# Splitting one VectorE product of a four-tile group into four products of one tile, in an edge-softmax kernel

## The reference, cut to what matters

```python
qkv = (h @ W_qkv + b_qkv).reshape(n, 3, H, DH)          # H = 8 heads of DH = 32
q, k, v = (qkv[:, 0], qkv[:, 1], qkv[:, 2])
score = jnp.einsum('ehd,ehd->eh', q[dst], k[src]) * SCALE
mx = jax.ops.segment_max(score, dst, num_segments=n)
ex = jnp.exp(score - mx[dst])
denom = jax.ops.segment_sum(ex, dst, num_segments=n)
attn = ex / denom[dst]
msg = attn[:, :, None] * v[src]
h_new = jax.ops.segment_sum(msg, dst, num_segments=n)
```

## Time and profile before

| | |
|---|---|
| time, median of 3 runs | 2125.84 us (2121.98 to 2130.7) |
| span of the profiled execution | 2134.3 us |
| stage with the attention's edges | about 1243 to 1900 us of the span |
| VectorE busy, share of the span | 72% |
| TensorE busy, share of the span | 83% |
| GpSimd busy, share of the span | 54% |

### The profile page before, as it was taken

The page is one execution under the profiler, slowest core; times in us unless marked ns, Lnnn a source line. Parts: engine busy times, 40 slices in busy tenths (PEclk is TensorE's granted clock), DMA queues, the critical chain, the costliest instruction groups (busy, mean ns, idle before and its releaser), DMA issues. The chain is left out here.

```text
span 2134.3 us, 41549 instructions
## 1 busy us (share of the span) xinstructions
PE 1761.5 (83%) x10388; PEld 1537.1 (72%) x10389; DVE 1539.6 (72%) x2788; ACT 1070.3 (50%) x2353; POOL 1160.5 (54%) x1169
## 2 busy tenths in 40 slices
PE   3699999999999989828973868888888888866278
PEld 3499999999999979728972756666666766645267
DVE  5388888888888845643545849899999898847622
ACT  1677777777777726403420145445455454316133
POOL 0376666666666601462443457777777777512112
PEclk7799999999999989758996989999999999867579
DMA  3443333333333312133323566666666666524310
GB/s 96 133 121 111 104 108 108 104 107 108 105 106 108 98 31 80 69 124 98 119 75 98 193 185 189 189 188 188 193 191 186 190 187 188 148 65 141 115 38 29
DMA packets 132538, 267.55 MB, mean 125 GB/s; under 512 B 24030, under 2 KB 75888, under 8 KB 132407
## 3 DMA queue, kind: packets, MB, share of 16 engines
q0 software_dynamic: 63456, 191.61, 30.7%
q1 hardware_dynamic: 68534, 73.21, 11.2%
q10 hardware_dynamic: 416, 1.18, 0.2%
HBM read 225.34 MB, written 42.50 MB: 125 GB/s over the span
## 5 line engine op out<-in xcount | busy, mean ns | idle before, releaser
L319 POOL DMA_INDIRECT e_rows<-h_table,e_idx x440 | 453.4, 1030 | 214.1 <-issue 106.3
L1740 POOL DMA_INDIRECT a_rows<-kv_table,a_idx x440 | 476.1, 1082 | 135.8 <-issue 128.9
L619 PE MATMUL e_w<-w2h,e_hidl 128*128 128x256 f32 x880 | 247.7, 304 | 2.9 <-DVE e_msg L704 2.9
L589 PE MATMUL e_agg<-e_msg,e_hot 128*128 128x256 f32 x880 | 246.1, 402 | 0.0
L1822 PE MATMUL a_q<-q,a_spread 128*128 x880 | 233.7, 407 | 6.5 <-ACT a_spread L1782 6.3
L620 PE MATMUL e_w<-w2l,e_hidh 128*128 128x256 f32 x880 | 226.4, 280 | 0.0
L1853 PE MATMUL a_agg<-a_rows,x 128*128 128x264 f32 x880 | 226.2, 402 | 0.0
L704 DVE TENSOR_TENSOR e_msg<-e_w,e_rows 128x1024 f32<-128x1024 f32 x110 | 134.7, 1224 | 93.4 <-PE e_w L623 93.4
L1775 ACT ACTIVATE a_apart<-iota_n,dst_rel 128x128 f32<-128x128 f32 x440 | 140.6, 391 | 112.9 <-PE a_agg L1853 112.8
L1822 PEld LDWEIGHTS a_q<-q,a_spread 128*128 128x128 f32 x880 | 166.2, 199 | 38.9 <-issue 12.8
L1853 PEld LDWEIGHTS a_agg<-a_rows,x 128*128 128x128 f32 x880 | 168.2, 200 | 24.7
(11 more groups left out here) (456 smaller groups left out, 4221.4 us busy)
## 6 DMA issues: line engine op xcount, KB each, us to landing
e_ea<-in_eaT SPq DMA_DIRECT2D x220, 64.0 KB
m_rows<-expert_rows SPq DMA_DIRECT2D x32, 272.0 KB, 2.7
e_rows<-h_table,e_idx POOLq DMA_INDIRECT x440
a_rows<-kv_table,a_idx POOLq DMA_INDIRECT x440, 3.7
q_ab<-expert_out SPq DMA_DIRECT2D x50, 128.0 KB, 3.3
kv_table<-q_kv SPq DMA_DIRECT2D x25, 256.0 KB, 2.2
u_stage<-in_m_w SPq DMA_DIRECT2D x16, 256.0 KB
x<-in_x SPq DMA_DIRECT2D x1, 3200.0 KB, 13.9
```

The costliest lines, as they stand in the source:

```text
L319: c.nc.gpsimd.indirect_dma_start(out=rows[:, g.slot8, j, :], out_offset=None, in_=table, in_offset=bass.IndirectOffsetOnAxis(ap=idx[:, g.s ...
L589: last = mm(bank(wins[j]), hot[:, g.slot4, t, :], msg[:, g.slot4, t, :], start=False, stop=False, skip_group_check=True)
L619: mm(w, hidl[:, g.slot, cols[k]], w2h[:, k, :], start=(k == 0), stop=False)
L1740: nc.gpsimd.indirect_dma_start(out=rows[:, g.slot * IG + j, 0:2 * D], out_offset=None, in_=c.kv_dram, in_offset=bass.IndirectOffsetOnAxis( ...
```

## The change

The one `tensor_tensor` over a group's four tiles (128 partitions x 4 x 256 elements) becomes a loop of four over one tile each (128 x 256). Operands, operation, type and place stay the same: it is in place, and the exponentials are read with a step of zero over the 32 elements of a head. The signal `s_msg` goes with the fourth. Nothing else is changed; lines behind it move down by four.

```diff
                         need(dve, s_dg, (s_ex, m.chunk + 1))
-                        ex = rows[:, four(m), 2 * D:ROW].rearrange("p t (h a) -> p t h a", a=1).broadcast_to([P, IG, H, DH])
-                        v.tensor_tensor(by_head(rows[:, four(m), D:2 * D]), by_head(rows[:, four(m), D:2 * D]), ex, ALU.mult).then_inc(s_msg, 1)
+                        for j in range(IG):
+                            tile = rows[:, m.slot * IG + j, :]
+                            values = tile[:, D:2 * D].rearrange("p (h d) -> p h d", h=H)
+                            ex = tile[:, 2 * D:ROW].rearrange("p (h a) -> p h a", a=1).broadcast_to([P, H, DH])
+                            last = v.tensor_tensor(values, values, ex, ALU.mult)
+                        last.then_inc(s_msg, 1)
                         ahead.fetch(i.then, "sums", m.n)
```

## The result

The changed kernel takes 2139.94 us in the median of 4 runs (2135.59 to 2141.53), against 2126.73 us (2121.98 to 2130.7, 4 runs) before: a ratio of 1.0059, 95% interval 1.0041 to 1.0077, so +12.5 us (8.7 to 16.4; the medians alone lie 13.2 us apart). The prediction was 2140 us, with 2130 to 2154 as its range.

A forecast was written before the change was run, and what follows sets the result against it. VectorE was taken to set the stage's pace, GpSimd close behind. 23.1 - 5.1 - 5.4 = +12.6 us, put at +14 for doubt in point 5; 2125.84 + 14 = 2140 us, range 2130 to 2154 us.

The forecast's parts named there:

- Points 1 to 3: VectorE's multiply in each group: three added instructions at 0.07 us each, 0.21 us a group, +23.1 us (20 to 26).
- Point 4: VectorE's wait for grow before L1903, once a chunk: the longer multiply covers it, -5.1 us.
- Point 5: VectorE's waits for gathered rows (all) and for queries and exponentials (half) go: -5.4 us (bounds 0 and -8.4).
- Point 6: TensorE's sums (L1848) come 0.21 us later each step; L1890 takes them later, so nothing new waits in the steady part.
- The period: Mean distance of the once-per-chunk marker L1928 (L1924 before): 22.8 to 22.9 us, against 22.34 us before.
- the stages ahead: Stages before and after the changed one: unchanged within 2 us in the profile.
- Rival A: Slack takes most of VectorE's added time; if all other waits vanished, a chunk takes 22.50 us: +4 to +10.6 us; 22%.
- Rival B: No overlap between the four multiplies on VectorE: durations count in full, +0.47 us a group, +47 us, 2173 us; 5%.
- Rival C: GpSimd falls behind if gathers are held through all four multiplies, not let in between: over +19, up to +30 us; 12%.
- the first reading: A gather meeting the first of four multiplies is held until the fourth ends; GpSimd needs 5.75 us a group, +18 us.
- Rival D: Faster: an added VectorE instruction costs under 0.04 us, freer gathers and covered waits outweigh it; down to -13 us, 2113 us; 4%.

The follow-up runs named there:

- the pair with fewer gathers: One multiply and four multiplies, each with the fourth tile of a group not gathered once the ring is full: -7.0 us and +12.3 us against before.
- light kernel: Kernel before, one multiply, with the fourth tile of a group not gathered once the ring is full (output partly wrong): 2121.2 us, ratio 0.9967.
- the move alone: Kernel before, one multiply, with the rescaling of the shared destination put behind the product of keys and queries: 2125.2 us, ratio 0.9992.
- two multiplies and the move: Against before: two multiplies of two tiles per group, and the rescaling put behind the product of keys and queries: 2112.93 us, ratio 0.9936.

## Why the prediction was right, step by step

- **Points 1 to 3, the price on VectorE** (0.21 us a group, 23.1 us): right. The trace shows 1.34 against 1.13 us, and eight multiplies fit the same 0.07 us per instruction.
- **Point 4, grow** (-5.1 us): right. The floor rose by 22.45 - 21.86 = 0.59 us and not by 4 x 0.21 = 0.84; in the pair with fewer gathers it rose by 0.69 (21.76 to 22.45). So 0.15 to 0.25 us per chunk were given back, and the forecast was 0.19. Price less grow was predicted as 18.0 us; that pair, in which almost no other wait is left to give, lies 19.3 us apart.
- **Point 5, the other waits** (-5.4 us): a good size, with a reason only half right. The light kernel shows that they were worth 7.0 us. I had said that only the waits for rows hang on the gathers, and had taken half of those for queries and exponentials by judgement. All but 0.5 us of them vanishes when gathers have room, even with VectorE as fast as before. I did not follow how a late gather turns into a wait for queries. For the exponentials the trace of before shows the way, over TensorE's clock. TensorE's matmul of L1811 waits once in a chunk for VectorE. Of 24 chunks, it waits 1.46 us or more in the 11 (1.20 or 1.21 us in 12 of the others) in which VectorE has waited for rows or queries just before. Behind 7 of these 11, and behind no other, the granted clock falls from full speed (2.4 GHz) to 0.50 of it (1.2 GHz) for about 4 us. The exponentials pass over TensorE next, and VectorE's 7 waits for them (3.1 us) are in these 7 chunks. One of them, TensorE's wait, its next eight matmuls, the clock in two windows (the third figure from the end), and VectorE's wait at the end:

```profile
1364.28 0.62 PE L1811 MATMUL a_misc<-carried,heads_of_row 8*128 8x34 f32 x2 [1.82 <-DVE carried L1941]
1364.83 3.42 PE L1822 MATMUL a_q<-q,a_spread 128*128 x8
```

```profile
1358.00:1363.00 5.00, 4.09 (x23) 3.11 (x21) 3.78 (x6) 2.68 (x9) 3.78 (x5) 1.00 0.61 184
1365.00:1367.00 2.00, 2.00 (x5) 1.64 (x6) 2.00 (x2) 0.00 (x0) 1.60 (x2) 0.50 0.73 219
```

```profile
1372.10 1.23 DVE L1896 TENSOR_TENSOR a_rows<-a_rows 128x1024 f32<-128x1024 f32 x1 [0.45 <-ACT a_rows L1761]
```

At full clock these eight matmuls take 1.99 us (at 1520.42). From 1300 to 1845 there are 7 falls and 7 waits for exponentials before, 12 and 11 with the move alone, 2 and 2 in the changed kernel, 1 and 1 with one multiply and fewer gathers, none of either with two multiplies and the move (read to 1830). That the late rows cause the falls is the likely reading, not a tested one: eight multiplies have 11 falls without any wait for rows, and none of these costs VectorE a wait.

- **Point 6** (nothing new waits): right. L1890 waits for no sums in the changed kernel.
- **The period** was forecast as 22.8 to 22.9 us and is 22.62. Over 25 chunks the profiles show +7.0 us, the whole stage +9.3, the timed runs +12.5; the steady chunks were over-estimated: their growth of 0.28 us, times 27.5, is 7.7 us, where the sum had 12.6. A single execution of each does not carry a statement of 3 us, but by the profiles the closeness of 12.5 to the forecast of 12.6 to 14 us is in part luck. That the stages ahead would agree within 2 us was wrong for the same reason (4.8 us).
- **Rival A** (slack takes most, +4 to +10.6 us) is less likely than the forecast by the timed runs and not excluded: their interval begins at 8.7 us, and the profiles' 7.7 to 9.3 us lie in its range. What it asked for, that all other waits end, nearly happened (8.4 us to 0.6); the mean chunk, 22.62 us, is 0.12 above the 22.50 that it named. **Rival B** falls with the starts 0.33 us apart: four pieces of 0.41 us take 1.41 us together. By its rule, in the Trainium skill's "VectorE: DVE Perf Modes", section "The DRAIN you can't avoid", the next one waits for an empty pipe; the trace does not agree for instructions that don't need each other's results. The same section adds that a next one that is not held starts earlier, which the prediction left out and the trace bears out.
- **Rival C** had two readings, and both happen. Of the gathers shown above, that at 1508.60 ends at 1509.69, 0.82 us after 1508.87, which is the end of the third piece (the pieces end about 0.42, 0.75, 1.09 and 1.42 us after the first one's start); that at 1503.23 begins under the first piece and ends at 1505.18, 0.84 us after the end of the fourth. By these four release times, 27 of the 100 delayed gathers were held to the end of the fourth though they began under an earlier one. The mean of 1.026 us lies between the two limits that I gave. What decides which of the two happens was not tested. (The sum for the first reading has a slip: 78 - 57 us over 99 groups is 0.21 us and not 0.19.) That an exclusive lock is given back after each instruction, as I read the Trainium skill's "SBUF — State Buffer", section "SBUF: two separate sides", agrees with the 73 others and not with these 27. Nor does a gather that gets in first hold the multiply for its whole 0.95 us: the multiply grows by 0.06 us at most.
- **Rival D** needed a price under 0.04 us and did not get it. But its mechanism, freer gathers that outweigh added work, is what two multiplies and the move point to.

What I had wrong was the picture of the kernel before: "VectorE sets the pace of this stage". It and the gathers did so together. Given time, VectorE alone would have run at 21.9 us per chunk, and the sign to read was in the earlier trace rows: GpSimd idles 0.30 us before each gather and never more. Counted over the stage, it pauses for longer than 0.35 us 0 times before and with the move alone, 11 times with two multiplies, 36 times with four, and 92 times with a quarter of the gathers left out. An engine that is never seen waiting for the others is not merely close behind.

## What to carry to other kernels

When two engines share the pace, work added to one is partly free and work taken from it brings little: before trusting a saving (the move, 0.4 us per chunk on VectorE by the floors 21.76 and 21.39 us, brought 1.7 us in all), lighten the other engine in an experiment and see whether the saving appears. Splitting one long two-input VectorE instruction costs the fixed 0.07 us for each added piece and shortens what GpSimd's gathers have to wait for; here two pieces were worth it once VectorE had been made fast enough, four were not. Put independent work between an instruction and the one that reads its result (0.22 us per place here), but not by delaying a signal on which another engine starts.

## What the runs showed of the hardware that was not expected

- A VectorE memset of 8 elements takes 0.02 us of the engine's time, a reduction of 8 elements 0.07 us, both without a wait between them and their neighbours.
- Behind a multiply in several pieces, a gather that was due under an early piece is sometimes released at the end of its piece, and sometimes (27 of 100 with four pieces) only at the end of the last.
- Whether a gather or the multiply goes first is decided within some hundredths of a us. In the kernel before, eight gathers that began from 0.02 us before the multiply to 0.03 us after it kept their 0.94 to 0.95 us, and the multiply took 1.23 to 1.28 us in place of 1.22. A ninth that also began 0.03 us after it, and all 15 that began 0.04 to 0.11 us after it, took 1.93 to 2.00 us and left the multiply as it was.
- Waits of VectorE for TensorE and ScalarE (5.9 us in the earlier trace rows) came down to 0.5 us when only GpSimd's gathers were thinned out. All 7 waits for exponentials stand behind stretches of about 4 us in which TensorE's granted clock was 0.50 (1.2 GHz).
